# Loading the cross-attention context in eight pieces along two later passes, in place of four pieces along one early pass

## The reference

```python
x = _layernorm(x + _L0_attn_ref(x, ...))                 # causal attention, 32 heads, 8 key/value heads, 4-bit weights, rotary embedding
x = _layernorm(x + _L0_xattn_ref(x, ctx_4096, ctx_4096, ...))   # 16 heads of 32 channels; softmax over sequences and heads
x = _layernorm(x + _L0_ffn_ref(x, ...))                  # main product plus gated low-rank experts
```

```python
def proj(x, W, bias):
    y = x @ W.T + bias
    return y.reshape(b, s, head_num, hd).transpose(0, 2, 1, 3).reshape(b * head_num, s, hd)
Q = proj(q, Wq, bq)
K = proj(k, Wk, bk)
V = proj(v, Wv, bv)
```

## Time and profile before

| | us |
|---|---|
| median of 3 runs | 686.75 |
| lowest and highest of them | 685.23, 690.6 |
| the profiled execution, whole time | 687.75 |
| its span, from first to last instruction | 686.0 |
| PE busy in the span | 641.8 (94%) |
| DVE, ACT, POOL busy | 557.7, 465.9, 420.7 |

### The profile page before, as it was taken

One profiled execution on the slowest core, in us unless ns is written; L12 is line 12 of the kernel. 1 busy time (PEld: TensorE's weight loads), 2 busy tenths in 40 slices (PEclk: granted clock), 3 DMA queues, 4 the chain that ended last, 5 costly groups with the idle time before them and its releaser, 6 DMA issues.

```text
span 686.0 us, 10990 instructions
## 1 busy us (share of the span) xinstructions
PE 641.8 (94%) x3293; PEld 446.4 (65%) x3294; DVE 557.7 (81%) x880; ACT 465.9 (68%) x1271; POOL 420.7 (61%) x372
## 2 busy tenths in 40 slices
PE   8889989999999999999999999999768998978996
PEld 4566767877778778787787777855544544447552
DVE  5878989998999999999899999953652977998347
ACT  5597877979779798797987978866623555722100
POOL 1578799899999989989989998871221000012003
PEclk9999999999999999999999999999989999999998
DMA  6865812532351351253244224230010000020003
GB/s 212 259 164 153 242 36 50 154 91 62 108 138 45 88 162 36 66 152 88 47 117 131 46 77 139 47 109 0 1 61 1 1 0 1 1 97 2 0 1 122
DMA packets 29611, 56.72 MB, mean 83 GB/s; under 512 B 4720, under 2 KB 4976, under 8 KB 29040
## 3 DMA queue, kind: packets, MB, share of 16 engines
q1 hardware_dynamic: 29552, 56.02, 28.8%
HBM read 32.93 MB, written 2.10 MB: 51 GB/s over the span
## 4 chain that ended last, share of the span: by engine, by line
PE 71%; DVE 9%; ACT 3%; issue 2%; POOL 2%; POOLq 0%; DVEq 0%; ACTq 0%
PE ps L1471 21%; PE ps L1526 16%; PE ps L1534 8%; PE ps L1486 7%; PE ps L1514 7%; PE ps L1496 4%; PE ps L1775 3%; DVE arena L1330 2%; ACT arena L989 1%; PE ps L1657 1%; DVE arena L1303 1%; DVE w_area L1311 1%; DVE late L1297 1%; DVE y L1251 1%; PE ps L1766 1%
## 5 line engine op out<-in xcount | busy, mean ns | idle before, releaser
L1105 DVE SCALAR_TENSOR_TENSOR arena<-ps,arena 128x512 f32<-128x512 f32 x288 | 212.6, 745 | 15.9 <-PE ps L1471 4.1
L1471 PE MATMUL ps<-x_hi,w_sb 128*128 128x512 f32 x384 | 171.5, 447 | 5.2 <-ACT arena L784 2.2
L1471 PE MATMUL ps<-x_lo,w_sb 128*128 128x512 f32 x384 | 151.6, 395 | 0.0
L1133 DVE SCALAR_TENSOR_TENSOR y<-ps,arena,y 128x512 f32<-128x512 f32 x192 | 138.8, 744 | 15.4 <-PE ps L1526 11.2
L1526 PE MATMUL ps<-heads_hi,wo_sb 128*128 128x512 f32 x256 | 110.0, 430 | 7.4 <-DVE y L1133 5.8
L793 ACT ACTIVATE arena<-ps,small 128x128 f32<-128x128 f32 x256 | 90.9, 378 | 27.9 <-DVE small L1111 27.9
L618 POOL TENSOR_TENSOR arena<-arena,consts 128x512 f32<-128x512 f32 x75 | 96.8, 1290 | 20.9 <-DVE arena L1105 20.9
L642 POOL TENSOR_TENSOR y<-arena,y 128x512 f32<-128x512 f32 x64 | 82.4, 1287 | 41.3 <-ACT arena L834 39.2
L624 POOL TENSOR_TENSOR arena<-arena,consts 128x512 f32<-128x512 f32 x75 | 96.7, 1289 | 17.2 <-DMA arena<-arena 16.0
L1526 PE MATMUL ps<-heads_lo,wo_sb 128*128 128x512 f32 x256 | 101.6, 397 | 0.0
L634 POOL TENSOR_TENSOR arena<-arena 128x512 f32<-128x512 f32 x75 | 96.6, 1288 | 5.6
(11 more groups left out here) (139 smaller groups left out, 970.2 us busy)
## 6 DMA issues: line engine op xcount, KB each, us to landing
arena<-arena SPq DMA_DIRECT2D x160, 128.0 KB, 2.3
arena<-in_qkv SPq DMA_DIRECT2D x48, 256.0 KB, 4.0
arena<-in_o SPq DMA_DIRECT2D x32, 256.0 KB, 3.8
arena<-in_x_t SPq DMA_DIRECT2D x8, 256.0 KB, 4.1
y<-in_x SPq DMA_DIRECT2D x4, 512.0 KB, 4.6
arena<-in_ctx_t SPq DMA_DIRECT2D x4, 512.0 KB, 6.4
out<-y SPq DMA_DIRECT2D x8, 256.0 KB, 2.1
arena<-in_wk SPq DMA_DIRECT2D x1, 1024.0 KB, 5.1
```

Source lines behind the costliest of these rows:

```text
L1105: nc.vector.scalar_tensor_tensor(acc, group_bank(p, KC * c + g), scale_of(p // 2, c, g), acc, ALU.mult, ALU.add).then_inc(dve_scaled, 1)
L1133: nc.vector.scalar_tensor_tensor(dst, by_tile(out_bank(p, u)), out_scale_of(p // 2, u), dst, ALU.mult, ALU.add).then_inc(out_added, 1)
L1471: mm = nc.tensor.matmul(group_bank(p, u), w_sb[:, c, g, :], part[:, g, half * HALF:(half + 1) * HALF], start=(k == 0), stop=(k == 1))
```

## The change

The four loads of the context in pass 1 go. In their place eight loads of 256 KB are issued: in pass 2 behind the turns of tiles 0, 2, 3 and 4 the first half of the tokens, for each of the four blocks of channels, and in pass 4 the second half in the same way. The wait of PE ahead of the last pass counts eight loads instead of four. Nothing else differs; the instructions of PE, DVE, ACT and POOL are the same, in the same order.

```diff
@@ first_phase(j), along pass 2j
                     turn(2 * j + 1, c)
                     if j == 0 and k < BPH:
                         sp.dma_start(y[:, 2 * k:2 * k + 2, :], t["x"][:, 2 * k:2 * k + 2, :]).then_inc(y_in, 16)
+                    if j in (1, 2) and k < KC:
+                        half = slice((j - 1) * HALF, j * HALF)
+                        sp.dma_start(ctx_t[:, k, half], t["ctx_t"][:, k, half]).then_inc(ctx_in, 16)
@@ second_phase(j), along pass 2j + 1
                     load_wo_piece(j + 1, k)
                     if j + 2 < NKV:
                         load_w_pieces(j + 2, W_PIECES[k])
-                    if j == 0 and k < KC:
-                        sp.dma_start(ctx_t[:, k, :], t["ctx_t"][:, k, :]).then_inc(ctx_in, 16)
@@ PE, ahead of phase(LAST)
-            pe.wait_ge(ctx_in, 16 * KC)
+            pe.wait_ge(ctx_in, 16 * 2 * KC)
```

## The result

The changed kernel takes 684.69 us (median of 20 runs, 683.49 to 686.91). The kernel before took 688.41 us in the 20 runs beside them (685.23 to 692.07). The ratio is 0.9945, with a 95% interval of 0.993 to 0.996: 3.8 us faster, between 2.8 and 4.8. The prediction was 684.4 us for the new kernel, by a gain of 2.35 us. That the time came out within 0.3 us of the forecast is partly luck: the median before, 688.41 us over more runs, lies 1.66 us above the 686.75 us that the forecast started from, and the gain by the medians, 3.72 us, is 1.37 us larger than forecast, so the two errors nearly cancel. The profiled execution took 684.61 us with a span of 682.8.

A forecast was written before the change was run, and what follows sets the result against it. PE was taken as the bound, busy 641.8 of 686.0 us. The profiled 687.75 us less 2.35 for pass 1, all other terms zero, gave 685.40; the median, 1.00 us lower, was forecast at 684.4, range 681.8 to 687.9.

The forecast's parts named there:

- What bounds: Whole kernel: PE's own work bounds normal passes; the one sizeable wait, 2.1 us for POOL, precedes pass 2's first scores.
- The cause of the wait: End of pass 1: POOL rotates late because the last turns land behind the context, the fifth after 4.5 and 5.2 us.
- Out of pass 1: Without context loads pass 1 runs like pass 3, 28.14 us instead of 30.49: gain 2.35 us, bounds 2.12 and 2.66.
- Into passes 2 and 4: Eight context pieces of 256 KB behind the first four turns of these passes: cost 0, upper end 3.9 us.
- The cover of 0.95 us: Even passes: the fifth turn can land 0.69 + 0.26 us later before PE's next first scores wait.
- The row of pass 3: A 256 KB weight piece issued 1.9 us before pass 3's fifth turn, which still landed within 2.2 to 2.4 us.
- the upper end of 3.9 us: Passes 2 and 4: cost if both fifth turns land 2.9 us later, less 0.95 us of cover each.
- What follows moves forward whole: From pass 2 on, everything including the tail shifts earlier by the full gain, since no transfer has a fixed time.
- The stall in the even passes: Rival: PE waits at the first scores of passes 3 and 5, costing 3.9 us, net +1.55, 688.3 us; 8 in 100.
- The gain did not stay away: Rival denied here: POOL is late in pass 1 by itself, PE waits as before, 686.7 us; 8 in 100.
- The clock of the tail: Rival: the half-clock dip at 501 to 508 us vanishes or repeats, 681.2 or 687.6 us; 10 in 100, half each side.
- theory B: Set up for the experiments, not the prediction: the gain beyond 2.35 us lies in the opening or the tail.

The follow-up runs named there:

- clump_pass2: Kernel before with all 2 MB of context moved to pass 2, 1 MB behind the third turn and 1 MB behind the fourth; ratio 0.9973.
- split_pass1: Kernel before with the context kept in pass 1 but cut into eight pieces of 256 KB, two behind each turn; ratio 1.0008.
- before_filled: Kernel before with eight unused products on PE right before the first scores of pass 2; 688.44 us, ratio 1.0005.
- last_two_late: Kernel before with the third and fourth context pieces of pass 1 moved behind its fifth turn; 685.07 us, ratio 0.9962.
- whole_pass2: Kernel before with the four whole 512 KB context pieces moved behind the turns of pass 2; 685.3 us, ratio 0.9948.
- after_filled: Changed kernel with eight unused products on PE right before the first scores of pass 2; 686.28 us, ratio 0.9975 against the kernel before.
- half_pass1: Kernel before with 256 KB of context behind each of the first four turns of pass 1, the other half in pass 4; ratio 0.997.

## Why the prediction was right

*What bounds.* Right: the one wait of the earlier trace rows was the one place where the change could act, and it went. But one sentence under it does not hold, that in the passes time goes when PE stands still, and hardly otherwise. PE counts as busy at half clock too, and in two of five profiles 1.5 to 1.6 us went that way. *The cause of the wait*, turns behind the context: right, and shown by moving nothing but the last two pieces behind the fifth turn, which brought the step of pass 1 to 28.09 us at unchanged traffic.

*Out of pass 1.* The new pass 1 was taken from pass 3: 28.14 us forecast, 28.11 measured; POOL 0.51 us early forecast, 0.65 measured. For the profiled execution the term of 2.35 us is 2.38. As the gain of the kernel it was too small: 2.35 us stands outside the interval of 2.8 to 4.8. The term that was mis-sized is "gain: 2.35 us, bounds 2.12 and 2.66". Its upper bound came from POOL's move alone, and I took one execution's loss for the loss. What it lacked is the clock behind the wait, 1.5 to 1.6 us in two of five profiles, and the scatter of the wait itself (1.78 to 2.46 us). I did weigh the clock, as a rival, but at the tail, where the earlier trace rows showed a fall. The same reasoning, PE idle and then slow, belonged to the 2.12 us of idle time that the change removes. The Trainium skill's page that I cited (TensorE: Matmul & The Clock Gate, "What's actually happening") says that the gate is not started anew with the kernel, from which I took that a fall can differ between executions without a change. The five profiles agree, with 1.13 us for the first scores in three and 2.03 to 2.05 in two.

*Into passes 2 and 4.* Forecast 0, measured steps of 28.42 and 28.44 against 28.41: right. The cover of 0.95 us was confirmed by the clumps. The row of pass 3 was the right neighbour, and the upper end of 3.9 us was far off, as whole pieces of 512 KB in pass 2 cost nothing either. *The smaller pieces:* nothing, right, by split_pass1. *What follows moves forward whole:* right from pass 2 to pass 14 (1.83 and 1.79 us).

*The rivals.* The stall in the even passes did not come. The gain did not stay away. The clock of the tail is real as scatter: in the new profile it stood at half from 496.6 to 503.4 us, before from 501 to 508, and the tail was 1.4 us shorter. This is the last of the signs that the prediction had named for being wrong, passes as forecast and a tail of another length. The other kernels do not tie it to the change: split_pass1 and before_filled, which keep the loss, have 251.95 and 252.09 us behind the last anchor, and last_two_late, which is free of it, has 253.71, against 251.23 in the new kernel.

What stays open: the middle of the measured gain (3.8 us) is above the 3.0 us of the five profiles. More such falls of the clock than two in five would close the gap, and so would chance in the interval of the ratio. Small waits for POOL in other odd passes (0.2 to 0.9 us in some traces of before and of the experiments, none in the new kernel's one) may have a part: from the anchor of pass 2 to that of pass 14 the five profiles of before took 339.6 us on the average, the new kernel, whole_pass2, last_two_late and after_filled 339.3. So may theory B. The five kernels with pass 1 free of the loss (those four and clump_pass2) took 251.2 to 253.7 us behind the last anchor, 252.2 on the average, and the seven profiles with the full 512 KB in front of each turn 252.0 to 253.8, on the average 252.8. But the opening went the other way, 63.6 against 62.9 us. All three differences are smaller than their scatter, and no run tells these apart.

## What to carry to other kernels

Behind a small transfer that an engine is about to need, look at what stands ahead of it in the same queue: two bulk pieces moved behind the last such transfer gave the pass its normal length, as moving the whole load to other passes did, with the same traffic (2.6 us faster, 1.1 to 4.1, against 3.8, 2.8 to 4.8; the two are not told apart). Cutting the pieces in halves gave nothing. And price a wait of PE of two microseconds by more than its length: the clock may fall in it or just behind it, so that a single profile shows the loss with or without that part, and several profiles are needed for its mean.

## What was not expected of the hardware

PE's granted clock fell to 0.50 behind a wait of only 1.78 us in a stretch in which PE was otherwise busy without a gap, and in another execution it stayed at 1.00 behind 2.46 us. The same choice shows in pass 0, behind a wait of PE of 2.2 us at about 41 us that both kernels have. In the new profile the clock was at half behind it, from 42.6 us on, 1.5 us after the wait had ended at 41.08 and PE worked again:

```profile
42.50:46.10 3.60, 3.60 (x9) 2.05 (x9) 2.37 (x5) 2.97 (x8) 2.99 (x4) 0.53 0.28 84
```

There the step from the anchor of pass 0 to that of pass 1 was 28.17 us; in all five profiles of the kernel before, where the clock stayed at full, it was 26.72 to 26.76, so this fall costs 1.4 us. Among the experiments it came in split_pass1, whole_pass2 and half_pass1 and stayed away in the other four, after_filled among them, whose work up to there is that of the new kernel. So I take it for chance, which thirteen traces do not prove. The new kernel's profile has thus lost 1.4 us in pass 0 that those of before had not, and gained in pass 1.
